# Swapping two returned parts of a KAN layer between TensorE's identity matmul and VectorE's sum

## The chip, the cores and the metric

The kernel runs on one core of one Trainium2 chip. The metric is the device time of one execution in microseconds (us). What is compared is the median over runs of the same kernel.

## The reference, cut to what matters

The program computes four layers in a row. The change lies in the third, a window layer made of "FastKAN" blocks over 8x8 windows of an image with 32 channels:

```python
def _fastkan(x, ln_g, ln_b, ws, wb, bb):
    ln = _layernorm(x, ln_g, ln_b)
    basis = jnp.exp(-((ln[..., None] - GRID) / DENOM) ** 2)      # 8 bases
    flat = basis.reshape(*basis.shape[:-2], -1)
    return flat @ ws.T + jax.nn.silu(x) @ wb.T + bb
y = _layernorm(wins, pn_g, pn_b)                                  # PN
a = y.reshape(b, WS, WS, c, S).transpose(0, 2, 3, 1, 4).reshape(b, WS * c, WS * S)
a = _fastkan(a, k1_ln_g, ...)                                     # K1
a = a.reshape(b, WS, c, WS, S).transpose(0, 3, 1, 2, 4).reshape(b, WS, WS, C)
d = y.reshape(b, WS, WS, c, S).transpose(0, 1, 3, 2, 4).reshape(b, WS * c, WS * S)
d = _fastkan(d, k2_ln_g, ...)                                     # K2
d = d.reshape(b, WS, c, WS, S).transpose(0, 1, 3, 2, 4).reshape(b, WS, WS, C)
e = _fastkan(y.reshape(b, WS * WS, C), k3_ln_g, ...).reshape(b, WS, WS, C)   # K3
z = a + d + e
z = _fastkan(z.reshape(b, WS * WS, C), k4_ln_g, ...).reshape(b, WS, WS, C)   # K4
out = z + wins
```

What matters here is `z = a + d + e`: the results of K1 and K2, which were computed in other layouts, are brought back and added to K3's.

## The kernel before, in words

The layer (`window_layer`) works on 64 tiles of 128 partitions x 2048 float32 values. Five engines run programs of their own, and each program is one static list. A table of positions at the top of the file (L1619 to L1642) gives each step of a tile a number; the steps of tile t stand at 128 t plus that number, and each engine issues its steps in the order of these sums. So several tiles are in flight: while K1, K2 and K3 of one tile are computed, K4 of the tile before is. One such period of 128 is called a round below.

In a round TensorE computes, for each of K1, K2, K3 and K4 in turn, eight basis products into the one accumulator `out` (`products`, L2144 to L2182). Some bases are ScalarE's exponentials (`ex`), the others are grown from them by VectorE with a multiplication by `ratio` (`grow`, L2018 to L2042). With the fifth product (`SILU_AT`) the silu part is added by four matmuls of 128x512 (L2173), and in K3, ahead of them, one of the two returned parts by four matmuls with the identity matrix (L2166). In the trace each 128x512 matmul of these is two records. Between the products stand the matmuls of the layer norms: centering (L2115, L2118), variance (L2128), spread (L2139).

K1 and K2 need their operands in other layouts. SyncE moves them by DMA from SBUF to SBUF, in eight transfers each: `feed_y` (L1812) brings the normed input into `kin`, `feed_u` (L1819) the silu operand into `ku`. K2's operands first pass a column-first copy on VectorE (`turn_y` L1958, `turn_u` L1963, tile `columns_first`). ScalarE evacuates K1's and K2's results over their silu operand in `ku` (`evacuate`, L1912), and `give_back` (L1828) moves them into B (`back_k1`, from K1) and D (`back_k2`, from K2). In B the columns are in the order of `out`. In D they are column-first: element (x, rw) of D belongs to element (rw, x) of `out`, with 8 x and 256 rw. The trace prints both as `back_k`; in the listing of the order, back_k_341 is B and back_k_335 is D.

After K3's last product, VectorE's `total` (L2007) adds three things into Z, K4's input: the accumulator, K3's bias, and the part that did not go through the identity matmul. Z, `out` and D are there read and written in D's order, so `out` and Z with a step of 8 elements.

All DMAs of the layer are SyncE's, in one list: besides the above, `load_x` (L1795, the next tile, from HBM), `load_r` (L1801, the tile again, for the residual) and `store` (L1806). Of the waits, these matter: `give_back` of K1 waits until K3's middle step of the tile before has read B, `give_back` of K2 until the total of the tile before has read D, both for their evacuation; `feed_u` waits until the last return of its kind has landed, since it overwrites what the return reads; K3's middle step waits for K1's return, the total for K2's.

Of the kernel before, what the change touches and what calls it, by code (L numbers as in the profile page):

```python
# [25 lines left out]
ALU = mybir.AluOpType  # L26
# [7 lines left out]
BAND = 8  # L34
BANDS = ROWS // BAND
TILE = BAND * COLS
BANK = 512
# [54 lines left out]
def wait_both(eng, sem_a, value_a, sem_b, value_b):  # L92

    value_a, value_b = (v if isinstance(v, int) else eng.to_reg(v) for v in (value_a, value_b))
    wait_past(eng, sem_a, value_a)
    wait_past(eng, sem_b, value_b)
# [1504 lines left out]
PN, K1, K2, K3, K4 = range(5)  # L1601
# [36 lines left out]
TANH, SILU = {PN: 231, K4: 449}, {PN: 241, K4: 452}  # L1638
TURN_Y, TURN_U, MEASURE = 230, 313, 633
LOAD_X, LOAD_R, STORE = 114, 552, 633  # L1640
FEED_Y, FEED_U, BACK = {K1: 218, K2: 235}, {K1: 261, K2: 328}, {K1: 365, K2: 421}
STAGES = 4  # L1642


# [34 lines left out]
def window_layer(net, k, source, bias, target, stats):  # L1679
    nc, c = net.nc, net.c  # L1680
# [11 lines left out]
    with ExitStack() as local:  # L1692
# [43 lines left out]
        def out_b(kind, h):  # L1736
            return k["end_b"][:, h:h + 1] if kind == K4 else vec[:, 3 * kind + 1:3 * kind + 2]

        def cols(n):
            return slice(BANK * n, BANK * n + BANK)  # L1740
# [4 lines left out]
        def after(t, first=1):  # L1745
            return not isinstance(t, int) or t >= first
# [38 lines left out]
        @block.sync  # L1785
        def _(sp):
            def chunks_first(tile_):
                return [tile_[:, cols(n)].rearrange("(g c) w -> c g w", g=GROUP) for n in range(CHUNKS)]

            def load_x(t, h):  # L1790
                pieces = chunks_first(source[band(t, h), h])
                if after(t):
                    sp.wait_ge(scaled[PN], t)
                for n in range(CHUNKS):
                    sp.dma_start(X[rows(n), :].rearrange("c (g w) -> c g w", g=GROUP), pieces[n]).then_inc(x_loaded, 16)  # L1795

            def load_r(t, h):
                pieces = chunks_first(source[band(t, h), h])
                wait_both(sp, stored, 16 * t, measured, t)
                for n in range(CHUNKS):  # L1800
                    sp.dma_start(R[rows(n), :].rearrange("c (g w) -> c g w", g=GROUP), pieces[n]).then_inc(r_loaded, 16)  # L1801

            def store(t, h):
                tile_ = target[band(t, h), h]
                sp.wait_ge(evacuated[K4], t + 1)
                sp.dma_start(tile_, R[:]).then_inc(stored, 16)  # L1806

            def feed_y(kind, t, h):
                wait_both(sp, normed if kind == K1 else copied_y, t + 1, exps, exps_done(kind, t - 1) if after(t) else 0)
                src = Y[:, h] if kind == K1 else turned[:]  # L1810
                for i in range(G):
                    sp.dma_start(kin[:, kind - K1, COLS * i:COLS * i + COLS],  # L1812
                                 src[P // G * i:P // G * i + P // G].rearrange("p (z n) -> p z n", z=BAND)).then_inc(kin_loaded[kind], 16)

            def feed_u(kind, t, h):
                wait_both(sp, u_ready[PN] if kind == K1 else copied_u, t + 1, back_loaded[kind], 128 * t)
                src = U[:, h] if kind == K1 else turned[:]
                for i in range(G):
                    sp.dma_start(ku[:, kind - K1, COLS * i:COLS * i + COLS],  # L1819
                                 src[P // G * i:P // G * i + P // G].rearrange("p (z n) -> p z n", z=BAND)).then_inc(ku_loaded[kind], 16)  # L1820

            def give_back(kind, t):
                if kind == K1:
                    wait_both(sp, used, BASES * slot_no(K3, t - 1) + (SILU_AT + 1) if after(t) else 0, evacuated[kind], t + 1)
                else:
                    wait_both(sp, summed, t, evacuated[kind], t + 1)
                for i in range(G):
                    sp.dma_start(back[kind][P // G * i:P // G * i + P // G].rearrange("p (z n) -> p z n", z=BAND),  # L1828
                                 ku[:, kind - K1, COLS * i:COLS * i + COLS]).then_inc(back_loaded[kind], 16)

            def round_(now):
                for u in range(UNITS):
                    for position, step in ((STORE, store), (LOAD_R, load_r), (LOAD_X, load_x)):
                        t, h = now.due(u, position)
                        if t is not None:
                            step(t, h)
                    for kind in (K1, K2):
                        t, h = now.due(u, FEED_Y[kind])
                        if t is not None:
                            feed_y(kind, t, h)  # L1840
                        t, h = now.due(u, FEED_U[kind])
                        if t is not None:
                            feed_u(kind, t, h)
                        t, h = now.due(u, BACK[kind])
                        if t is not None:
                            give_back(kind, t)
            rounds(sp, round_)
            sp.wait_ge(stored, 16 * TILES)
# [97 lines left out]
        def _(dve):  # L1946
            v = nc.vector

            def columns_first(tile_):
                return tile_.rearrange("p (x rw) -> p x rw", x=BAND)  # L1950

            def rows_first(tile_):
                return tile_.rearrange("p (rw x) -> p x rw", x=BAND)
# [48 lines left out]
            def total(t, h):  # L2002
                if after(t):
                    dve.wait_ge(exps, exps_done(K4, t - 1))
                dve.wait_ge(back_loaded[K2], 128 * t + 128)
                dve.wait_ge(used, BASES * slot_no(K3, t) + BASES)
                v.scalar_tensor_tensor(rows_first(Z[:]), rows_first(out_flat), out_b(K3, h), columns_first(D[:]), ALU.add,  # L2007
                                       ALU.add).then_inc(summed, 1)

            def measure(t, h):  # L2010
                dve.wait_ge(evacuated[K4], t + 1)
# [67 lines left out]
        def _(pe):  # L2079
# [63 lines left out]
            def products(kind, n, t, h):  # L2143
                if n == 0:  # L2144
                    last = slot_no.before(kind, t)
                    if last is not None:
                        pe.wait_ge(summed if last[0] == K3 else evacuated[last[0]], last[1] + 1)
                if n == SILU_AT:
                    if kind in (K1, K2):
                        pe.wait_ge(ku_loaded[kind], 128 * t + 128)  # L2150
                    else:
                        pe.wait_ge(u_ready[PN if kind == K3 else K4], t + 1)
                    if kind == K3:
                        pe.wait_ge(back_loaded[K1], 128 * t + 128)
                    elif kind == K4:
                        pe.wait_ge(r_loaded, 64 * t + 64)
                if n in ANCHORS[kind]:
                    pe.wait_ge(exps, exps_due)
                    pe.reg_add(exps_due, exps_due, 1)
                else:  # L2160
                    pe.wait_ge(grown, grown_due)
                    pe.reg_add(grown_due, grown_due, 1)
                if n == SILU_AT:
                    if kind == K3:
                        for i in range(CHUNKS):
                            m.matmul(out[:, i, :], c["ident"][:], B[:, cols(i)], start=False, stop=False)  # L2166
                    elif kind == K4:
                        for i in range(CHUNKS):
                            for g in range(GROUP):
                                m.matmul(out[rows(g), i, :], k["grown"][rows(i), h, rows(g)], R[rows(i), cols(g)],  # L2170
                                         start=False, stop=False, tile_position=(QUAD * i, QUAD * g))
                    for i in range(CHUNKS):
                        m.matmul(out[:, i, :], k["kan_silu"][:, kind - 1, :], silu_of(kind, h)[:, cols(i)], start=False, stop=False)  # L2173
                if n in ANCHORS[kind]:
                    base = ex[:, ANCHORS[kind].index(n)]
                else:
                    base = grown_ex[:, GROWTHS[kind].index(n) % GROWN]
                for i in range(CHUNKS):
                    for g in range(GROUP):
                        last = m.matmul(out[rows(i), g, :], k["kan_basis"][rows(g), kind - 1, n, :], base[rows(g), cols(i)],  # L2180
                                        start=(n == 0), stop=(n == BASES - 1), tile_position=(QUAD * g, QUAD * i))
                last.then_inc(used, 1)  # L2182
# [359 lines left out]
```

## Time and profile before

| | us |
|---|---|
| median of 3 runs | 10815.07 |
| lowest, highest | 10814.88, 10825.75 |
| the profiled execution: span from its first to its last instruction | 10821.2 |
| busy in it: TensorE | 8878.0 |
| VectorE | 8891.7 |
| ScalarE | 8014.9 |

A device time is listed for the runs and a span for the profiled execution; the span is what stands for that execution's own time here, and it lies among the three runs. The window layer's totals run from 4535 us to 10002 us of this span. Before it lie the two convolution layers with the residual and the pole layer, after it the pattern layer.

### The profile page before, as it was taken

To read this page: it belongs to the slowest core of one execution; us is meant where nothing else is said; L and a number is where in the kernel's file an instruction comes from. 1 tells how busy PE (TensorE), PEld (TensorE's weight loads), DVE (VectorE), ACT (ScalarE), POOL (GpSimd) and SP (SyncE) were. 2 spreads that over 40 slices of the span, in tenths; PEclk is the share of its full clock that TensorE was granted. 3 is DMA by queue.
4 is the path that set the end of the run, shared out by engine and by line. 5 is a ranking of instruction groups with operands and counts; after the bars stand their busy time and mean duration, and the time that the engine had idled before them with its cause. 6 is when DMAs were issued, how large, how long until landed. Compare 5 with 4: busy or idle time off the path is not lost. (4 is left out here: it accounts for less than half of the span.)

```text
span 10821.2 us, 354779 instructions
## 1 busy us (share of the span) xinstructions
PE 8878.0 (82%) x158376; PEld 4547.3 (42%) x158376; DVE 8891.7 (82%) x9022; ACT 8014.9 (74%) x5451; POOL 0.2 (0%) x4
## 2 busy tenths in 40 slices
PE   0889879996665799588888888888888888888788
PEld 0344434433442688244444444444344444443444
DVE  6777756666777588699999999999999999998788
ACT  0555545554552555599999999999999999998788
POOL 0000000000000000000000000000000000000000
PEclk9999989998887999699999999999999999999899
DMA  7999979996663588355444454555445455554576
GB/s 286 247 257 260 240 217 263 266 264 211 267 274 120 155 279 277 77 115 111 110 107 111 107 111 107 115 119 112 111 107 111 107 111 115 119 110 93 173 211 195
DMA packets 1196555, 1825.76 MB, mean 169 GB/s; under 512 B 135328, under 2 KB 956448, under 8 KB 1124768
## 3 DMA queue, kind: packets, MB, share of 16 engines
q1 hardware_dynamic: 1195040, 1803.05, 61.9%
q8 instruction: 1257, 20.59, 0.8%
q14 instruction: 258, 2.11, 0.1%
HBM read 717.78 MB, written 411.04 MB: 104 GB/s over the span
## 5 line engine op out<-in xcount | busy, mean ns | idle before, releaser
L2042 DVE SCALAR_TENSOR_TENSOR grown_ex<-ratio,ex 128x2048 f32<-128x2048 f32 x768 | 1756.1, 2287 | 229.7 <-PE out L2180 162.1
L2180 PE MATMUL out<-grown_ex,kan_basis 32*32 32x512 f32 x40960 | 1691.9, 625 | 7.7 <-DVE grown_ex L2042 5.4
L556 PE MATMUL conv<-uc,w 128*32 128x512 f32 x12288 | 1445.6, 596 | 15.4 <-DMA uc<-u 15.4
L1902 ACT ACTIVATE ex<-ex 128x2048 f32<-128x2048 f32 x768 | 1447.6, 1901 | 4.2
L2180 PE MATMUL out<-ex,kan_basis 32*32 32x512 f32 x24576 | 1233.3, 660 | 256.5 <-ACT ku L1912 156.5
L2042 DVE SCALAR_TENSOR_TENSOR grown_ex<-ratio,grown_ex 128x2048 f32<-128x2048 f32 x512 | 1171.2, 2288 | 27.4 <-PE out L2180 21.3
L463 ACT ACTIVATE v<-conv,cb 128x512 f32<-128x512 f32 x512 | 350.8, 685 | 899.6 <-PE conv L556 388.3
L2180 PEld LDWEIGHTS out<-grown_ex,kan_basis 32*32 32x32 f32 x40960 | 590.6, 106 | 731.1 <-issue 631.5
L1898 ACT ACTIVATE ex<-kin,offset 128x2048 f32<-128x2048 f32 x384 | 758.6, 1991 | 128.4 <-PE out L2180 127.8
L556 PEld LDWEIGHTS conv<-uc,w 128*32 128x32 f32 x12288 | 498.0, 109 | 715.7 <-issue 667.9
L2319 DVE TENSOR_TENSOR d<-xt 128x2313 f32<-128x2313 f32 (+2 forms) x256 | 621.7, 2495 | 88.2 <-PE acc L2373 87.9
L2373 PE MATMUL acc<-d,weights 32*32 32x512 f32 x16384 | 626.6, 599 | 73.3 <-issue 67.4
L2180 PEld LDWEIGHTS out<-ex,kan_basis 32*32 32x32 f32 x24576 | 419.6, 107 | 613.3 <-issue 532.5
L2139 PE MATMUL norm<-q,c_sel 32*128 32x128 f32 x10240 | 461.5, 328 | 171.5 <-ACT x L1863 136.6
L2139 PEld LDWEIGHTS norm<-q,c_sel 32*128 32x128 f32 x10240 | 391.8, 226 | 481.7 <-ACT x L1863 195.5
L2341 ACT ACTIVATE d<-d,steep 128x2313 f32<-128x2313 f32 (+2 forms) x256 | 534.0, 2159 | 35.3 <-DVE d L2319 35.3
L660 DVE TENSOR_TENSOR u<-xn,spread 128x512 f32<-128x512 f32 (+2 forms) x320 | 379.3, 1218 | 165.7 <-PE spread L521 163.5
L2128 PE MATMUL norm<-sq,c_kan_ones 128*32 128x128 f32 x10240 | 362.0, 281 | 176.3 <-ACT y L1865 76.0
L2173 PE MATMUL out<-ku,kan_silu 128*128 128x512 f32 x1024 | 472.6, 605 | 1.5 <-DVE grown_ex L2042 1.5
L2128 PEld LDWEIGHTS norm<-sq,c_kan_ones 128*32 128x32 f32 x10240 | 271.5, 112 | 464.8 <-issue 197.0
L2373 PEld LDWEIGHTS acc<-d,weights 32*32 32x32 f32 x16384 | 319.5, 103 | 327.7 <-issue 216.5
L1898 ACT ACTIVATE ex<-z,offset 128x2048 f32<-128x2048 f32 x192 | 383.2, 1996 | 54.5 <-PE out L2180 44.0
(287 smaller groups left out, 16012.2 us busy)
## 6 DMA issues: line engine op xcount, KB each, us to landing
uc<-u SPq DMA_DIRECT2D x2048, 129.0 KB, 3.5
xt<-in_x SPq DMA_DIRECT2D x128, 1024.0 KB, 7.3
t<-v SPq DMA_DIRECT2D x128, 1024.0 KB, 9.7
back_k<-ku SPq DMA_DIRECT2D x1024, 128.0 KB, 4.0
xt<-in_x SPq DMA_DIRECT2D x32, 2048.0 KB, 7.8
xt<-t SPq DMA_DIRECT2D x64, 1024.0 KB, 6.6
tt<-t SPq DMA_DIRECT2D x64, 1024.0 KB, 12.1
x<-x SPq DMA_DIRECT2D x64, 1024.0 KB, 4.9
```

Source lines behind the costliest of these rows:

```text
L556: last = m.matmul(conv[QUAD * b:QUAD * b + QUAD, k % 2, :], w_sb[:, o, d, :], uc[:, h, b, 2 * p:2 * p + 2, d:d + COLS], start=(d == 0), st ...
L660: return v.tensor_tensor(inside(u[:, h, first_row:first_row + rows, 1:COLS + 1]), inside(xn[:, h, at].rearrange("p (r w) -> p r w", w=COLS ...
L1898: a.activation(ex[:, j], norm_out(kind, h), ACT.Square, bias=k["offset"][:, kind - 1, n:n + 1]).then_inc(args, 1)
L1902: a.activation(ex[:, j], ex[:, j], ACT.Exp, scale=-1.0).then_inc(exps, 1)
L2042: v.scalar_tensor_tensor(grown_ex[:, at % GROWN], ratio[:], LARGEST, below, ALU.min, ALU.mult).then_inc(grown, 1)
L2128: last = m.matmul(norm[rows(quarter), 0, 0:P], k["c_kan_ones"][:, 0 if kind in (K1, K2) else 1, i, :], sq[:, block_:block_ + P], start=(i ...
L2139: last = m.matmul(norm[:, quarter, P * i:P * i + P], k["c_sel4"][rows(quarter), i, :], q[group][rows(quarter), group.index(kind), :], star ...
L2173: m.matmul(out[:, i, :], k["kan_silu"][:, kind - 1, :], silu_of(kind, h)[:, cols(i)], start=False, stop=False)
L2180: last = m.matmul(out[rows(i), g, :], k["kan_basis"][rows(g), kind - 1, n, :], base[rows(g), cols(i)], start=(n == 0), stop=(n == BASES - ...
L2319: v.tensor_tensor(d[:, h, n, rows, columns], there, xt[:, parity, h, rows, columns], ALU.subtract).then_inc(diff_ready, 1)
L2341: a.activation(t, t, ACT.Tanh, scale=steep[:, h:h + 1]).then_inc(tanh_ready, 1)
L2373: last = m.matmul(acc[quad(k), h, g, :], weights[quad(g), n, :], source_tile[quad(g), row + 2 * k:row + 2 * k + 2, column:column + COLS], ...
```

## The change

The two returned parts change places. K2's part (D) is now added inside K3 by the identity matmul, whose moving operand reads D with a step of 256 elements between neighbouring columns, so that its order becomes that of `out`. K1's part (B) is added by VectorE's total, in which all operands are now contiguous. The waits are exchanged accordingly, and K2's return gets position 383 in place of 421.

```diff
-FEED_Y, FEED_U, BACK = {K1: 218, K2: 235}, {K1: 261, K2: 328}, {K1: 365, K2: 421}
+FEED_Y, FEED_U, BACK = {K1: 218, K2: 235}, {K1: 261, K2: 328}, {K1: 365, K2: 383}
...
             def give_back(kind, t):
                 if kind == K1:
+                    wait_both(sp, summed, t, evacuated[kind], t + 1)
+                else:
                     wait_both(sp, used, BASES * slot_no(K3, t - 1) + (SILU_AT + 1) if after(t) else 0, evacuated[kind], t + 1)
-                else:
-                    wait_both(sp, summed, t, evacuated[kind], t + 1)
...
             def total(t, h):
...
-                dve.wait_ge(back_loaded[K2], 128 * t + 128)
+                dve.wait_ge(back_loaded[K1], 128 * t + 128)
                 dve.wait_ge(used, BASES * slot_no(K3, t) + BASES)
-                v.scalar_tensor_tensor(rows_first(Z[:]), rows_first(out_flat), out_b(K3, h), columns_first(D[:]), ALU.add,
-                                       ALU.add).then_inc(summed, 1)
+                v.scalar_tensor_tensor(Z[:], out_flat, out_b(K3, h), B[:], ALU.add, ALU.add).then_inc(summed, 1)
...
                     if kind == K3:
-                        pe.wait_ge(back_loaded[K1], 128 * t + 128)
+                        pe.wait_ge(back_loaded[K2], 128 * t + 128)
...
                     if kind == K3:
+                        by_rows = D[:].rearrange("p (x rw) -> p rw x", x=BAND)
                         for i in range(CHUNKS):
-                            m.matmul(out[:, i, :], c["ident"][:], B[:, cols(i)], start=False, stop=False)
+                            m.matmul(out[:, i, :], c["ident"][:], by_rows[:, BANK // BAND * i:BANK // BAND * i + BANK // BAND, :],
+                                     start=False, stop=False)
```

SyncE's list in a steady round, before (x at L1806 is the layer's output in HBM, written by the store; back_k_341 is K1's return, back_k_335 K2's):

```order
L1812 DMA kin<-columns_first 128x1x256 x8
L1828 DMA back_k_341<-ku 16x8x256 x8
L1795 DMA x<-x 32x4x512 x4
L1806 DMA x<-x_to_x_332 128x2048
L1819 DMA ku<-silu_y 128x1x256 x8
L1828 DMA back_k_335<-ku 16x8x256 x8
```

and now:

```order
L1812 DMA kin<-columns_first 128x1x256 x8
L1828 DMA back_k_341<-ku 16x8x256 x8
L1795 DMA x<-x 32x4x512 x4
L1806 DMA x<-x_to_x_332 128x2048
L1828 DMA back_k_335<-ku 16x8x256 x8
L1819 DMA ku<-silu_y 128x1x256 x8
```

K2's return has moved ahead of the feed of K1's silu operand for the next tile, and is directly behind the store. After both, in each list, comes the load for the residual.

TensorE's list around K3's middle step, with the semaphores that a row waits for, before (grown: a basis of VectorE's is ready; back_loaded1: K1's return has landed; u_ready0: the silu operand is ready; exps: an exponential is ready):

```order
L2128 MATMUL norm<-sq,c_kan_ones 32x128 x15
L2162 REGISTER_ALU [waits grown_394,back_loaded1_414,u_ready0_405]
L2166 MATMUL out<-back_k_341,c_ident 128x512 x4
L2173 MATMUL out<-silu_y,kan_silu 128x512 x4
L2180 MATMUL out<-grown_ex,kan_basis 32x512 x16
```

and now (back_loaded2: K2's return has landed):

```order
L2127 MATMUL norm<-sq,c_kan_ones 32x128 x15
L2161 REGISTER_ALU [waits grown_394,back_loaded2_415,u_ready0_405]
L2166 MATMUL out<-back_k_335,c_ident 128x512 x4
L2174 MATMUL out<-silu_y,kan_silu 128x512 x4
L2181 MATMUL out<-grown_ex,kan_basis 32x512 x16
```

The place of the identity matmuls is the same; the return that they wait for, and the tile that they read, are the other ones.

## Rows read from the trace of the kernel before

**Rows 1.** The page's head and busy time by engine.

```profile
span 10821.2 us, 354779 instructions
...
PE 8878.0 (82%) x158376; PEld 4547.3 (42%) x158376; DVE 8891.7 (82%) x9022; ACT 8014.9 (74%) x5451; POOL 0.2 (0%) x4
```

**Rows 2.** One line's view: L2007, the total; ns min/median/max, first and last start.

```profile
L2007 DVE SCALAR_TENSOR_TENSOR z<-out,kan_vec,back_k x64: 3893/3946/3999, 4535.0 to 9998.1; 128x2048 f32<-128x2048 f32 x64
```

**Rows 3.** Timeline of VectorE, one round: start us, us, what, idle before.

```profile
7019.58 2.03 DVE L1958 COPY columns_first<-y 128x2048 f32<-128x2048 f32 x1
...
7050.07 2.29 DVE L2042 SCALAR_TENSOR_TENSOR grown_ex<-ratio,ex 128x2048 f32<-128x2048 f32 x1 [1.68 <-PE out L2180]
...
7055.01 3.94 DVE L2007 SCALAR_TENSOR_TENSOR z<-out,kan_vec,back_k 128x2048 f32<-128x2048 f32 x1 [0.39 <-ACT ex L1902]
...
7072.31 2.29 DVE L2042 SCALAR_TENSOR_TENSOR grown_ex<-ratio,ex 128x2048 f32<-128x2048 f32 x1 [0.31 <-PE out L2180]
...
7104.77 2.03 DVE L1958 COPY columns_first<-y 128x2048 f32<-128x2048 f32 x1
```

**Rows 4.** Windows, second round: busy time by engine, granted clock, DMA share, GB/s.

```profile
7996.00:8001.00 5.00, 4.71 (x51) 2.52 (x52) 3.92 (x6) 4.47 (x4) 0.00 (x0) 0.66 0.99 326
```

**Rows 5.** Timeline of TensorE in the second round.

```profile
7996.29 1.09 PE L2180 MATMUL out<-ex,kan_basis 32*32 32x512 f32 x16 [2.02 <-issue]
7997.31 1.94 PE L2128 MATMUL norm<-sq,c_kan_ones 128*32 128x128 f32 x32
7999.18 4.45 PE L2166 MATMUL out<-back_k,c_ident 128*128 128x512 f32 x8
```

**Rows 6.** Timeline of VectorE in the second round.

```profile
7974.89 2.03 DVE L1958 COPY columns_first<-y 128x2048 f32<-128x2048 f32 x1
...
8009.48 2.29 DVE L2042 SCALAR_TENSOR_TENSOR grown_ex<-ratio,ex 128x2048 f32<-128x2048 f32 x1 [5.11 <-PE out L2180]
```

**Rows 7.** Timeline of TensorE in the first round.

```profile
7039.51 1.08 PE L2128 MATMUL norm<-sq,c_kan_ones 128*32 128x128 f32 x32 [0.42 <-ACT sq L1872]
7040.52 3.70 PE L2166 MATMUL out<-back_k,c_ident 128*128 128x512 f32 x8
...
7058.11 1.65 PE L2139 MATMUL norm<-q,c_sel 32*128 32x128 f32 x32 [2.19 <-ACT x L1863]
7059.68 2.01 PE L2180 MATMUL out<-ex,kan_basis 32*32 32x512 f32 x32
...
7083.48 3.70 PE L2173 MATMUL out<-ku,kan_silu 128*128 128x512 f32 x8
```

**Rows 8.** Timeline of SyncE's issues in the first round.

```profile
7021.64 5.15 SPq L1812 DMA_DIRECT2D kin<-columns_first  x8
7026.89 5.44 SPq L1828 DMA_DIRECT2D back_k<-ku  x8
7032.37 3.40 SPq L1795 DMA_DIRECT2D x<-x  x4
7035.81 0.43 SPq L1806 DMA_DIRECT2D x<-x_to_x  x1
7036.34 8.39 SPq L1819 DMA_DIRECT2D ku<-silu_y  x8
```

**Rows 9.** Lines' views: K1's return from 7026.8, then the silu feed's last issue.

```profile
DMA to landing us min/median/max: 3.3/3.4/4.4
...
L1819 SPq DMA_DIRECT2D ku<-silu_y x1: 599/599/599, 7044.1 to 7044.1; - x1
...
DMA to landing us min/median/max: 3.8/3.8/3.8
```

**Rows 10.** Timeline of ScalarE: K2's evacuation in the first round.

```profile
7030.15 1.96 ACT L1912 ACTIVATE ku<-out,kan_vec 128x2048 f32<-128x2048 f32 x1
```

**Rows 11.** Groups by line and shape, 5000 to 9800 us: busy, mean ns, idle before.

```profile
L1991 DVE SCALAR_TENSOR_TENSOR kin<-kin,kan_vec,norm 128x2048 f32<-128x2048 f32 x110 | 257.4, 2340 | 0.0
...
L1958 DVE COPY columns_first<-y 128x2048 f32<-128x2048 f32 x56 | 113.8, 2032 | 0.0
```

## The prediction, made before the changed kernel ran

> **What bounds the kernel now.** I read the profile in this order: the page, to see which engines fill the span; the single line of the instruction that the change rewrites; one round of the layer on SyncE, on TensorE, on VectorE and on ScalarE; then a second round, in which chance delayed TensorE.
>
> The span is 10821.2 us, and TensorE and VectorE are each busy for 82% of it [rows 1]. The change touches the KAN stage alone. Its 64 totals start between 4535.0 and 9998.1 us [rows 2], so a round lasts (9998.1 - 4535.0) / 63 = 86.7 us on average. The round that I read is a quiet one: VectorE's column-first copy starts at 7019.58 and again at 7104.77 [rows 3], 85.2 us later. In it VectorE is nearly always at work, with a wait of 1.68 us ahead of 7050.07 as the longest in the rows shown, and that wait ends on TensorE's K3 products [rows 3]. So inside this stretch TensorE is already the later of the two, by 1.68 us, and anything that delays TensorE ahead of that point reaches VectorE in full.
>
> The second round shows this happening. TensorE stood still for 2.02 us at 7996.29 before it reached K3's middle step. It then ran at a lower granted clock (0.66 over 7996 to 8001, so partly at 1.2 GHz), the variance matmuls took 1.94 us and the four identity matmuls (eight records) 4.45 us, and VectorE waited 5.11 us where it otherwise waits 1.68 [rows 4 to 6]. The quiet round has 3.70 us for the same identity matmuls [rows 7]. From the end of the column-first copy to the identity matmuls are 7999.18 - 7976.92 = 22.26 us there and 7040.52 - 7021.61 = 18.91 us in the quiet round [rows 3, 5, 6, 7]: TensorE came 3.35 us later, and VectorE's wait grew by 3.43 us.
>
> **The change, part by part.**
>
> 1. K3's middle step now needs K2's return, not K1's. K1's return starts at 7026.89, is issued in 5.44 us, and its eight transfers land 3.3 to 4.4 us after issue [rows 8, 9], all of them by 7032.3 + 4.4 = 7036.7, which is 3.8 us ahead of the identity matmuls at 7040.52. K2's part is far later: ScalarE's evacuation of it runs from 7030.15 to 7032.11 [rows 10]. It is then ready, but SyncE is not. SyncE's chain starts when VectorE's column-first copy ends (7021.61) and runs without a pause: K2's feed 5.15 us, K1's return 5.44, the load of x 3.40, the store 0.43 [rows 8]. Even at its new, earlier place K2's return is issued no sooner than 7036.3. Today the feed of K1's silu operand stands exactly there, with the same eight transfers of 128 KB: SyncE takes 8.39 us to issue them, behind the megabyte load and the megabyte store, and the last one, issued at 7044.1, lands 3.8 us later, at 7047.9 [rows 8, 9]. I price K2's return by this row, since it will stand in the same queue behind the same work. TensorE would be kept 7047.9 - 7040.5 = 7.4 us. The average round is 1.5 us longer than this one, largely because TensorE arrives late in some, and there the stall hides as much; I take 1.0 us off: **+6.4 us** a round. Bounds: with the eight issues at the 5.44 us of K1's return and 3.4 us of landing the last arrives at 7045.1, a stall of 4.6, and 3.6 with the same 1.0 off; with a landing 2 us later than the row, 8.4.
> Nothing can be put in the stall's place: TensorE takes its instructions in order, and behind the wait stand K3's silu matmuls, its last four products, the spread for K2 and x's centering. The step from the identity matmuls to VectorE's release is 7050.07 - 7040.52 = 9.55 us of unbroken TensorE work [rows 3, 7].
>
> 2. The clock. After the chance gap of 2.02 us the variance matmuls took 0.86 us longer than the 1.08 of the quiet round and the identity matmuls 0.75 us longer [rows 5, 7]: 1.6 us of loss behind a gap that is a third of the new stall. **+1.6 us** a round; bounds 0 and 3.2 (twice that, if the lower clock lasts twice as long).
>
> 3. The identity matmuls themselves. Their moving operand now steps by 256 elements (1 KB) from one column to the next. No matmul of the trace reads so. The nearest row is VectorE's column-first copy, which reads SBUF with a step of 8 elements: 2032 ns for 2048 elements, about 1 ns each, less than the 2340 ns of the contiguous form below [rows 11]. TensorE takes 3.70 us for 8 x 512 columns, 0.9 ns each, nearly the same pace, so I take **0**. Bounds: 0 (it cannot be quicker than the contiguous read) and 3.7, a doubling.
> The Trainium skill ("SBUF — State Buffer", in the section on the DMA port swizzle) says that SBUF is read in lines of 16 bytes and that each access that crosses to a new line pays a penalty. The copy row does not bear this out for VectorE; no run here shows it for TensorE, and by that rule the upper bound would be the value to take.
>
> 4. VectorE's total. It reads PSUM and writes Z with a step of 8 elements today; plain and contiguous it should cost what the scale step costs, one PSUM operand and one SBUF operand in 2340 ns [rows 11]; it takes 3.94 us today [rows 3]. That is 1.6 us of VectorE's time a round. Most of it is not on the path. The total ends at 7055.01 + 3.94 = 7058.95, while TensorE's next work waits for ScalarE's x until 7058.11, then spreads for 1.65 us, and opens K4 at 7059.68 [rows 3, 7]. VectorE waits again for TensorE's K4 products at 7072.31, 0.31 us [rows 3]. An earlier end of the total would mostly lengthen that wait. **-0.4 us** a round; bounds 0 and -1.6.
>
> 5. SyncE. K2's return moves ahead of K1's silu feed and of R's load; both keep their number of transfers, and the silu feed now lands some 6 us later. It is needed only at K1's middle step of the next tile, whose silu matmuls start at 7083.48 [rows 7], near 30 us after it lands, so I put 0 on it. The exchanged waits of the two returns (the last total, the last middle step of K3) are both from the tile before and long past: 0.
>
> Sum: 6.4 + 1.6 + 0 - 0.4 = 7.6 us a round, times 64 tiles = 486 us. On the profiled execution's 10821.2 us that is 11307; this execution's span lies 6 us above the median of the three runs, 10815.07, so against the median it is 11301, and I say **11300 us**.
>
> **Rivals.**
>
> A. *K2's return lands in time, and the change is faster.* The mechanism: the return goes out the moment that ScalarE has evacuated K2, at 7032.1. Eight issues at 0.65 us and 3.4 us of landing end at 7040.7, within 0.2 us of the identity matmuls. It decides at a landing 18.9 us after the copy's end. Then only the total's gain is left, 0.4 to 1.6 us a round: 26 to 103 us, 10712 to 10790. Against it stand the load of x and the store, which hold SyncE until 7036.3 [rows 8]. Chance 0.05.
>
> B. *The strided operand costs as well.* Doubling the identity matmuls adds 3.7 us x 64 = 237 us to the forecast: 11537. Against it is the copy row; for it, that the step is 1 KB and no row has that on TensorE. It is the time that the Trainium skill's rule on SBUF lines would give. Chance 0.2.
>
> C. *The stall is absorbed.* If the rounds had slack elsewhere (SyncE's chain starting earlier against TensorE, ScalarE running ahead), the stall would show only as a longer wait and the time would stay within 0.2%, about what a measurement of this kernel can tell from no change. The second round speaks against it: 3.35 us of delay came out as 3.43 us of waiting. Chance 0.04, with 10795 to 10835.
>
> D. *The forecast*, a stall of 4 to 8 us a round and little else: chance 0.71.
>
> **How the numbers follow.** The low end takes a stall of 3.6 us, a clock loss of 1.6 and a gain of 0.4: 4.8 x 64 = 307, so 11120. The high end takes 8.4 + 3.2 less 0.4, or 6.4 + 1.6 + 3.7 for rival B with its price: 11.2 to 11.7 x 64 = 717 to 749, so 11560. What lies outside is A, C and a slim tail above. Faster by more than 0.2% has A's 0.05, within 0.2% C's 0.04, slower the rest, 0.91.
>
> **What the changed profile would show.** Right: rounds of 93 to 96 us; TensorE idle 5 to 8 us before the identity matmuls, ended by the DMA of K2's return; VectorE's wait before K4's first growth 8 to 10 us in place of 1.68; a total of about 2.34 us; the granted clock at its lower level behind the stall; the window's DMA work unchanged. The identity matmuls stay at 3.7 us (5.3 with the lower clock) if the stride is free. Wrong: K2's return landing less than 19 us after the copy; identity matmuls of 7 us at the full clock; or a stall on TensorE without longer rounds.

## The result, and the profile after

| | before | changed |
|---|---|---|
| median, us | 10814.97 (4 runs) | 11641.49 (4 runs) |
| lowest to highest | 10807.23 to 10825.75 | 11621.33 to 11646.12 |
| ratio | | 1.0757, 95% interval 1.0737 to 1.0776 |

The change costs 826 us, 12.9 us for each of the 64 tiles. The direction was as forecast; the size was 1.7 times the forecast 485 us, and the time lies above the stated range. In the sessions of the experiments below the kernel before had medians of 10815 to 10847 us, so each experiment is read by its ratio to the kernel before in its own session.

The page of the changed kernel: head, busy time, the two groups that grew, and the issues of the returns (size, median us to landing).

```profile
span 11644.3 us, 354779 instructions
...
PE 9107.5 (78%) x158376; PEld 4588.8 (39%) x158376; DVE 8795.3 (76%) x9022; ACT 8016.7 (69%) x5451; POOL 0.2 (0%) x4
...
L2041 DVE SCALAR_TENSOR_TENSOR grown_ex<-ratio,ex 128x2048 f32<-128x2048 f32 x768 | 1756.4, 2287 | 1043.3 <-PE out L2181 988.2
...
L2166 PE MATMUL out<-back_k,c_ident 128*128 128x512 f32 x512 | 463.5, 1061 | 603.2 <-issue 603.2
...
back_k<-ku SPq DMA_DIRECT2D x1024, 128.0 KB, 8.9
```

VectorE is 96 us less busy than in [rows 1], which is the cheaper total, and the kernel is 826 us slower. Its growths from an exponential (L2041) now wait 1043 us, 988 of them for TensorE, where they waited 230. The identity matmuls are preceded by 603 us of idle TensorE; and TensorE itself is busy for 230 us more, 64 x 3.6 us.

One round on SyncE, in answer to [rows 8]:

```profile
7093.32 5.15 SPq L1812 DMA_DIRECT2D kin<-columns_first  x8
7098.57 6.71 SPq L1828 DMA_DIRECT2D back_k<-ku  x8
7105.32 2.04 SPq L1795 DMA_DIRECT2D x<-x  x4
7107.40 0.43 SPq L1806 DMA_DIRECT2D x<-x_to_x  x1
```

K2's return follows at 7107.95, 14.6 us after the end of the column-first copy (7093.30), as forecast. The line's view of single issues of that return, first and last, and of the silu feed behind it, first and seventh:

```profile
L1828 SPq DMA_DIRECT2D back_k<-ku x1: 552/552/552, 7108.0 to 7108.0; - x1
DMA to landing us min/median/max: 8.6/8.6/8.6
...
L1828 SPq DMA_DIRECT2D back_k<-ku x1: 598/598/598, 7114.7 to 7114.7; - x1
DMA to landing us min/median/max: 7.8/7.8/7.8
...
L1819 SPq DMA_DIRECT2D ku<-silu_y x1: 601/601/601, 7115.4 to 7115.4; - x1
DMA to landing us min/median/max: 7.1/7.1/7.1
...
L1819 SPq DMA_DIRECT2D ku<-silu_y x1: 607/607/607, 7119.3 to 7119.3; - x1
DMA to landing us min/median/max: 5.6/5.6/5.6
```

The last transfer of the return lands 7.8 us after its issue, at 7122.5, where the silu feed that stood in this place before landed 3.8 us after its own [rows 9]. The eight returns land between 7116.6 and 7122.5, one every 0.84 us. The feed's first seven land between 7122.5 and 7124.9, one every 0.40 us; its eighth, issued at 7120.0, takes 6.6 us and lands at 7126.6.

TensorE in that round, in answer to [rows 7]:

```profile
7111.97 1.08 PE L2127 MATMUL norm<-sq,c_kan_ones 128*32 128x128 f32 x32 [0.42 <-ACT sq L1872]
7122.87 7.24 PE L2166 MATMUL out<-back_k,c_ident 128*128 128x512 f32 x8 [9.82 <-issue]
7129.93 3.61 PE L2174 MATMUL out<-silu_y,kan_silu 128*128 128x512 f32 x8
```

VectorE, in answer to [rows 3]:

```profile
7091.26 2.04 DVE L1958 COPY columns_first<-y 128x2048 f32<-128x2048 f32 x1
...
7135.96 2.29 DVE L2041 SCALAR_TENSOR_TENSOR grown_ex<-ratio,ex 128x2048 f32<-128x2048 f32 x1 [15.11 <-PE out L2181]
...
7140.89 2.35 DVE L2007 SCALAR_TENSOR_TENSOR z<-out,kan_vec,back_k 128x2048 f32<-128x2048 f32 x1 [0.38 <-ACT ex L1902]
...
7149.12 2.29 DVE L2041 SCALAR_TENSOR_TENSOR grown_ex<-ratio,grown_ex 128x2048 f32<-128x2048 f32 x1 [1.48 <-PE out L2181]
```

TensorE idles 9.8 us, and VectorE waits 15.1 us where it waited 1.7. The total takes 2.35 us instead of 3.94, and the third growth behind it, which had no wait in the round read before, now waits 1.48 us for TensorE: nearly all of the 1.6 us saved is given back at once.

The windows over the stall (us, busy by engine with counts, granted clock, DMA share, GB/s):

```profile
7112.00:7116.00 4.00, 1.05 (x32) 0.78 (x32) 3.74 (x3) 3.52 (x2) 0.00 (x0) 1.00 1.02 335
7116.00:7120.00 4.00, 0.00 (x0) 0.00 (x0) 3.45 (x8) 3.95 (x3) 0.00 (x0) 0.67 1.13 163
7120.00:7124.00 4.00, 1.13 (x2) 0.62 (x3) 0.77 (x2) 3.54 (x2) 0.00 (x0) 0.50 1.11 251
7124.00:7128.00 4.00, 4.00 (x6) 1.43 (x5) 0.00 (x0) 0.00 (x0) 0.00 (x0) 0.55 1.08 227
7128.00:7132.00 4.00, 4.00 (x8) 1.37 (x7) 0.00 (x0) 0.00 (x0) 0.00 (x0) 1.00 0.37 74
```

While the return lands (7116 to 7120) the DMA engines are occupied throughout and move only 163 GB/s; and the first 5 us of the identity matmuls fall under a granted clock near 0.5, which is 1.2 GHz.

### The profile page after: what moved, and what is told of

Its sections match the earlier page's. It is cut to its first block and busy times, and to the rows that moved or that the text cites. A ratio compares the mean times of both kernels' runs of the same rounds, so it can differ in the third digit from the quotient of the medians.

```text
span 11644.3 us, 354779 instructions
## 1 busy us (share of the span) xinstructions
PE 9107.5 (78%) x158376; PEld 4588.8 (39%) x158376; DVE 8795.3 (76%) x9022; ACT 8016.7 (69%) x5451; POOL 0.2 (0%) x4
## 5 line engine op out<-in xcount | busy, mean ns | idle before, releaser
L2041 DVE SCALAR_TENSOR_TENSOR grown_ex<-ratio,ex 128x2048 f32<-128x2048 f32 x768 | 1756.4, 2287 | 1043.3 <-PE out L2181 988.2
L2041 DVE SCALAR_TENSOR_TENSOR grown_ex<-ratio,grown_ex 128x2048 f32<-128x2048 f32 x512 | 1170.8, 2287 | 120.3 <-PE out L2181 115.6
L2166 PE MATMUL out<-back_k,c_ident 128*128 128x512 f32 x512 | 463.5, 1061 | 603.2 <-issue 603.2
L2166 PEld LDWEIGHTS out<-back_k,c_ident 128*128 128x128 f32 x512 | 140.3, 289 | 837.0 <-issue 837.0
```

The costliest lines, as they stand in the source:

```text
L2041: v.scalar_tensor_tensor(grown_ex[:, at % GROWN], ratio[:], LARGEST, below, ALU.min, ALU.mult).then_inc(grown, 1)
L2166: m.matmul(out[:, i, :], c["ident"][:], by_rows[:, BANK // BAND * i:BANK // BAND * i + BANK // BAND, :], start=False, stop=False)
```

## The experiments

Two readings carry the comparison. *Arrival* is the time from the end of VectorE's column-first copy to the first identity matmul. *Release* is the time from there to the start of VectorE's first K4 growth. Both, and the *round* (total to total), are means over tiles 3 to 61 of the timelines of each run's profile.

| kernel | arrival | identity matmuls | release | round | time, us | ratio to before (95%) |
|---|---|---|---|---|---|---|
| before | 20.0 | 3.8 | 9.7 | 86.9 | 10815 | |
| changed | 29.5 | 7.2 | 13.1 | 99.9 | 11641 | 1.076 (1.074 to 1.078) |
| e1 return at 366 | 22.9 | 7.2 | 13.0 | 93.3 | 11246 | 1.039 (1.037 to 1.041) |
| e6 return at 371 | 27.2 | 7.2 | 13.1 | 97.6 | 11505 | 1.061 (1.056 to 1.067) |
| e7 return at 421 | 32.5 | 7.2 | 13.1 | 103.0 | 11843 | 1.093 (1.087 to 1.099) |
| e5 return shaped as a feed | 26.0 | 7.2 | 13.1 | 96.3 | 11418 | 1.053 (1.048 to 1.059) |
| e2 operand plain | 29.5 | 5.8 | 11.6 | 98.6 | 11558 | 1.068 (1.066 to 1.070) |
| e8 at 366, operand plain | 22.7 | 4.9 | 10.7 | 91.0 | 11112 | 1.025 (1.019 to 1.031) |
| e3 before, operand strided | 19.9 | 7.2 | 13.0 | 90.2 | 11048 | 1.021 (1.019 to 1.023) |
| e4 before, total plain | 19.8 | 3.8 | 9.7 | 86.6 | 10816 | 0.999 (0.998 to 1.000) |
| e12 before, step of 16 bytes | 19.9 | 7.5 | 13.3 | 90.6 | 11075 (one run) | |
| e11 before, step of 8 bytes | 20.0 | 3.9 | 9.8 | 87.2 | 10864 (one run) | |

In every row the round is 86.9 plus what arrival and release have above 20.0 and 9.7, to within 0.4 us: the changed kernel, 86.9 + 9.5 + 3.4 = 99.8 against 99.9; e8, 86.9 + 2.7 + 1.0 = 90.6 against 91.0. Next to nothing is left over for the total. Where TensorE waits for the return (the changed kernel, e1, e2, e5 to e8), its last landing lies 0.1 to 0.2 us ahead of the arrival, both as means of each run's trace, so the arrival is that landing. e9 and e10 move the identity matmuls behind two more products; the two readings mean something else there, and they stand below and not in the table.

The theory after the result, as the expectations below call it, is **S**: a late return and a slow operand are two separate costs, each in full on the path. Its rivals (the letters are not those of the prediction): **C**, that the 7.2 us of the identity matmuls are the lower clock; **V**, that VectorE's total counts; **Q**, that only the queue ahead makes the return late.

**e1, the return ahead of the load and the store.**

```diff
-... BACK = ..., {K1: 365, K2: 383}
+... BACK = ..., {K1: 365, K2: 366}
```

> The changed kernel with one number altered: K2's return at position 366 instead of 383, so directly behind K1's return and ahead of the load of x and of the store. Theory S (the lateness of the return and the strided operand are two separate costs): the last transfer lands 20.5 to 21.5 us after the end of the column-first copy instead of 29.3, TensorE's gap before the identity matmuls falls from 9.7 us to 0.5 to 2, the identity matmuls stay at 7.24 us; a round of 90.5 to 92 us, a time of 11050 to 11150 us. Theory C (the 7.24 us are the lower clock after the gap and the stride is free): with the gap gone the identity matmuls are back at 3.7 us and the time is 10830 to 10900 us.

Timeline of TensorE, then of SyncE, one round:

```profile
7053.85 7.21 PE L2166 MATMUL out<-back_k,c_ident 128*128 128x512 f32 x8 [3.89 <-issue]
```

```profile
7029.71 5.15 SPq L1812 DMA_DIRECT2D kin<-columns_first  x8
7034.96 12.75 SPq L1828 DMA_DIRECT2D back_k<-ku  x16
7047.75 2.04 SPq L1795 DMA_DIRECT2D x<-x  x4
```

The arrival falls from 29.5 to 22.9 us and the identity matmuls stay at 7.2, which speaks against C. It does not settle it: a gap of 3.2 us on average is left, and the granted clock over these matmuls is still 0.77 on average. e3 settles it. The arrival is later than the 21.5 us that I allowed and the time 96 us above S's range: 16 returns in a row take longer than I allowed (on average K2's eight are issued over 5.3 us and land over 6.6). A place ahead of K1's return was not tried. K2's evacuation ends 10.5 us after the copy [rows 3, 10] and its return starts 11.4 us after it here, so that place could start it at most some 0.9 us sooner.

**e2, the stride taken out of the changed kernel** (K2's part is then added in the wrong column order).

```diff
-    m.matmul(out[:, i, :], c["ident"][:], by_rows[:, ...], ...)
+    m.matmul(out[:, i, :], c["ident"][:], D[:, cols(i)], ...)
```

> The changed kernel with D read contiguously by the identity matmuls (K2's part is then added in the wrong column order). All waits and all DMAs stay. Theory S: TensorE's gap stays at 9 to 10 us; the lower clock, which in the changed kernel covers about the first 5 us after the gap, becomes visible, so the identity matmuls take 5 to 6.5 us; time 11520 to 11600 us. Theory C: the stride cost nothing, so the identity matmuls stay at 7.2 us and the time at 11640 us.

TensorE, one round:

```profile
7093.06 6.07 PE L2166 MATMUL out<-back_k,c_ident 128*128 128x512 f32 x8 [10.35 <-issue]
```

The stall stays, the matmuls take 5.8 us on average and the time falls by 83 us, inside S's range. So behind a stall the lower clock costs 5.8 - 3.8 = 2.0 us. In the changed kernel it costs nothing more, because the strided matmuls take 7.24 to 7.25 us in every round from tile 3 to 61, though their granted clock is 0.69 on average. The two costs overlap.

**e3, the stride alone, in the kernel before** (K1's part in the wrong column order): the identity matmuls read B as the change reads D.

> The kernel before, with one edit: the identity matmuls read B with the step of 256 elements (K1's part is then added in the wrong column order). Nothing waits for anything else than before. Theory S: the identity matmuls take 7.2 us instead of 3.7 in every round, at the full clock too, and all of it is on the path: (7.24 - 3.70) x 64 = 227 us, time 11020 to 11060 us. Theory C: the stride is free, 10815 us.

The line's view of the identity matmuls (ns min/median/max), and under it the same view before:

```profile
L2167 PE MATMUL out<-back_k,c_ident x512: 1041/1044/1223, 4530.1 to 10209.7; 128*128 128x512 f32 x171
```

```profile
L2166 PE MATMUL out<-back_k,c_ident x512: 590/593/1223, 4521.1 to 9985.9; 128*128 128x512 f32 x171
```

With no stall and no changed wait the stride costs 3.3 us a round and 2.1% of the time. In 53 of the 59 rounds from tile 3 to 61 the full clock was granted over all of these matmuls, and there they take 7.2 us. So C falls.

**e4, the total alone, in the kernel before** (K2's part in the wrong column order).

```diff
-    v.scalar_tensor_tensor(rows_first(Z[:]), rows_first(out_flat), out_b(K3, h), columns_first(D[:]), ...)
+    v.scalar_tensor_tensor(Z[:], out_flat, out_b(K3, h), D[:], ...)
```

> The kernel before, with one edit: the total reads the accumulator and D and writes Z contiguously (K2's part is then added in the wrong column order). Theory P (the total is not on the path): the total takes 2.35 us instead of 3.95, VectorE waits for TensorE's first K4 products instead, and the time falls by 0 to 25 us. Theory V (VectorE is the bound): it falls by 1.6 x 64 = 102 us, to 10713 us.

The line's view, then the waits between 5400 and 9600 us (us in total, times, longest), here and before:

```profile
L2007 DVE SCALAR_TENSOR_TENSOR z<-out,kan_vec,back_k x64: 2345/2350/2352, 4541.3 to 9982.6; 128x2048 f32<-128x2048 f32 x64
```

```profile
DVE grown_ex L2041 <- PE out L2179: 211.0, 143, 6.4
```

```profile
DVE grown_ex L2042 <- PE out L2180: 145.5, 107, 5.7
```

VectorE saves 1.6 us a round in work and waits 66 us more over some 48 rounds, 1.4 us each. The time is the same within the interval, so V falls.

**e5, the return with a feed's shape.** Each of its eight transfers reads 16 partitions and writes 128, the other way about (D's arrangement is then another).

```diff
-    sp.dma_start(back[kind][P // G * i:P // G * i + P // G].rearrange("p (z n) -> p z n", z=BAND),
-                 ku[:, kind - K1, COLS * i:COLS * i + COLS])
+    sp.dma_start(D[:, COLS * i:COLS * i + COLS],      # K2 alone
+                 ku[P // G * i:P // G * i + P // G, 1].rearrange("p (z n) -> p z n", z=BAND))
```

> The changed kernel, K2's return still at 383, but each of its eight transfers now reads 16 partitions and writes all 128, as a feed does, instead of reading 128 and writing 16 (D then holds K2's part in another arrangement). Number, size (128 KB) and row length (1 KB) of the transfers stay. Theory W (the return is slow by its own shape; in the changed kernel one of its transfers lands every 0.80 us, one of the silu feed's every 0.40): the spacing falls to 0.4 to 0.5 us and the last one lands 25.5 to 27 us after the column-first copy instead of 29.3; TensorE's gap is 6.5 to 7.5 us, the time 11400 to 11500 us. Theory Q (only the queue ahead of it, with the load of x and the store, makes it late): no change, 11640 us.

TensorE, one round:

```profile
7023.57 7.24 PE L2170 MATMUL out<-back_k,c_ident 128*128 128x512 f32 x8 [6.81 <-issue]
```

The arrival falls by 3.5 us at the same place in the queue, with the same bytes in rows of the same length, so Q falls as the sole cause. As means over tiles 3 to 59, the first of the eight transfers lands 22.2 us after the copy and the last 25.8; in the changed kernel it is 23.3 and 29.3. So 1.1 us of the 3.5 lie ahead of the first landing and 2.4 in the pace of the eight: the first seven land 0.40 us apart here and 0.80 there. Whether it is the reading of 128 partitions or the writing of 16 that is slow was not separated.

**e6 and e7, other places for the return.** 371 is between the load of x and the store, 421 the old place.

> The changed kernel with K2's return at position 371: behind the load of x, ahead of the store. With 366 (ahead of both) the last transfer landed 22.7 us after the column-first copy, with 383 (behind both) 29.3. Theory Q2 (each of the two megabytes ahead costs about its own transfer time): 25.5 to 26.5 us, a time of 11400 to 11470 us. Rival (the store alone does it): 23 to 24 us and 11250 to 11320 us.

> The changed kernel with K2's return left at its old position, 421, behind the feed of K1's silu operand. This is the exchange without the move. Theory S (each us of landing later is a us of the round): the last transfer lands 33 to 37 us after the column-first copy, the round grows to 104 to 108 us and the time to 11900 to 12150 us. Rival (the rounds have slack that takes up a longer stall): under 11750 us.

The line's view of the returns' issues between 7000 and 7110 us, at 371 and then at 421 (in both stretches only K2's return has landings on record).

```profile
DMA to landing us min/median/max: 6.5/7.1/7.5
```

```profile
DMA to landing us min/median/max: 3.3/3.4/3.6
```

In these two rounds a transfer takes 7.1 us to land behind the megabyte load and 3.4 behind the silu feed. Over 5400 to 9600 us the medians are 7.6 and 4.0, so the second round is a quick one: on average e7's eight returns are issued over 4.7 us and land over 6.0.

The arrival is 22.9 us ahead of both large transfers, 27.2 behind the load, 29.5 behind both, 32.5 behind the silu feed too. By these differences the load of x costs 4.3 us, more than I gave it, and the store 2.3; e6 missed my range upward by 35 us, e7 missed it downward by 57, since the silu feed costs only 3.0. The new place that came with the change saves 1.6% against leaving the return where it was (1.093 to 1.076), and every place tried is slower than before.

**e8, early and plain together** (K2's part in the wrong column order).

> The changed kernel with K2's return at 366 and D read contiguously (K2's part is then added in the wrong column order): the exchange with its stride removed and its lateness cut to what two returns in a row need. Theory S: TensorE's gap stays near 3.2 us, the identity matmuls take 4 to 6 us (part of them at the lower clock), the round 90.5 to 92 us, the time 11050 to 11150 us: still slower than before, since the total's 1.6 us are not on the path. Theory V (the total's 1.6 us count once TensorE no longer loses time to the stride): 10950 us or less.

Inside S's range. The exchange loses 2.5% even without its stride, from 2.7 us of later arrival and 1.0 us of lower clock.

**e9, the need made later.** e1's kernel with K3's middle step at the seventh product instead of the fifth.

```diff
-    SILU_AT = BASES // 2
+    SILU_AT = {K1: BASES // 2, K2: BASES // 2, K3: BASES // 2 + 2, K4: BASES // 2}
```

> The changed kernel with K2's return at 366 and K3's middle step (its wait for the return, the identity matmuls and the silu matmuls) moved from its fifth to its seventh product. Two products of about 0.9 us each then run before the wait. Theory S: TensorE's gap falls from 3.2 to about 1.4 us and that is gained in each round: 91.3 to 92 us, time 11120 to 11180 us, still slower than before by the stride's 3.4 us a round. Rival (VectorE's wait only moves to the spread behind the seventh product, and the sum of the path stays): 11246 us as with 366 alone.

11117.53 us, ratio 1.025 (1.022 to 1.029) against 1.039 in e1, and just below S's range. TensorE's gap falls to 0.6 us. It is the fastest form of the exchange found that adds every part in its right order, and still slower than before.

**e10, the same edit in the kernel before**, meant as a version faster than both.

> The kernel before with the same edit: K3's middle step at the seventh product instead of the fifth. TensorE does the same work in the same total time; only the sixth product, which releases VectorE's first K4 growth, comes 7.3 us earlier. Theory M (what VectorE needs next is the spread behind the seventh product, at the same time as before): 0 to 20 us faster. Rival N (the wait of 1.7 us before the growth is what bounds the round): up to 1.7 x 64 = 109 us faster, 10706 us.

Wrong for both theories: 10955.35 us, ratio 1.010 (1.007 to 1.013). VectorE, one round:

```profile
6564.06 2.29 DVE L2042 SCALAR_TENSOR_TENSOR grown_ex<-ratio,ex 128x2048 f32<-128x2048 f32 x1 [0.98 <-ACT ex L1902]
...
6567.93 2.35 DVE L1991 SCALAR_TENSOR_TENSOR kin<-kin,kan_vec,norm 128x2048 f32<-128x2048 f32 x1 [1.57 <-PE norm L2139]
...
6570.92 3.98 DVE L2007 SCALAR_TENSOR_TENSOR z<-out,kan_vec,back_k 128x2048 f32<-128x2048 f32 x1 [0.65 <-ACT ex L1902]
```

In place of the waits of 1.68 and 0.39 us [rows 3] stand three, of 3.2 us together, and the identity matmuls start 24.2 us after the copy, on average, where two products more should have made it 21.8. In that stretch TensorE is idle for 3.7 us on average, against 2.9 before, and its granted clock is 0.96 against 0.99. One reading is that the 7.3 us of identity and silu matmuls were cover under which ScalarE and VectorE made K3's next bases, and that they cover nothing once they are moved behind. It is argued from these rows and not shown.

**e11 and e12, how large a step costs.** The kernel before, with the identity matmuls reading B with a step of 2 and of 4 elements (K1's part in the wrong column order).

```diff
-    m.matmul(..., B[:, cols(i)], ...)
+    m.matmul(..., B[:].rearrange("p (n s) -> p s n", s=2)[:, i // 2, cols(i % 2)], ...)      # e11
+    m.matmul(..., B[:].rearrange("p (n s) -> p s n", s=4)[:, i, :], ...)                     # e12
```

> The kernel before with the identity matmuls reading B with a step of 2 elements, 8 bytes (K1's part is then added in the wrong column order). Theory L (a read pays when consecutive elements lie in different lines of 16 bytes): two elements share a line, so 3.7 to 4.0 us for the identity matmuls and 10815 us. Theory T (any step but 1 pays): 7.2 us and about 11040 us.

> The kernel before with the identity matmuls reading B with a step of 4 elements, 16 bytes (K1's part is then added in the wrong column order). Theory L: each element lies in a line of its own, so 7.2 us and about 11040 us, as with a step of 1 KB. Rival (only large steps pay): 3.7 us, 10815 us.

The line's view of each, step 8 bytes and then 16:

```profile
L2166 PE MATMUL out<-back_k,c_ident x512: 609/611/1222, 4528.7 to 10016.9; 128*128 128x512 f32 x171
```

```profile
L2166 PE MATMUL out<-back_k,c_ident x512: 1078/1079/1250, 4530.4 to 10237.8; 128*128 128x512 f32 x171
```

593 ns contiguous, 611 at 8 bytes, 1079 at 16 bytes, 1044 at 1 KB: the cost comes between 8 and 16 bytes and is no larger at 1 KB. Steps between these were not run.

## Why the prediction was right or wrong

**The bound and the mechanism of the stall: right.** TensorE stands still at K3's middle step until K2's return has landed; VectorE waits for it; each us of it is a us of the round. Four places of the return (e1, e6, the change, e7) show it over arrivals of 22.9 to 32.5 us. The prediction's rivals A (the return lands in time) and C (the stall is absorbed) fall with that. Its rival B (the strided operand costs as well) came true on top of the stall.

**Step 1, the stall: the term was mis-sized.** I put 6.4 us with 8.4 as the upper bound; it is 9.5. The start of the return, 14.6 us after the copy, was right, and so was the 1.0 us taken off for the rounds in which TensorE arrives late: the arrival before is 20.0 us on average and 18.9 in the round that I read. Wrong was "I price K2's return by this row, since it will stand in the same queue behind the same work": the row was a feed. A return has the same bytes and the same number of transfers but goes from 128 partitions to 16. With a feed's shape at the same place the arrival is 3.5 us earlier (e5), which covers the 3.1 us by which I missed. K1's return stood in my own rows with 3.4 us from issue to landing, and the low bound and rival A took it as the price of a return; but it had no large load and store ahead of it, and that round was a quick one: as means over tiles 3 to 59 before, its eight transfers are issued over 5.1 us, land over 6.5, and the last takes 5.0 us.

**Step 2, the clock: right in size, wrong in the sum.** A stall costs 2.0 us of lower clock with a plain operand (e2), against 1.6 forecast. In the changed kernel it is covered by the stride.

**Step 3, the strided operand: wrong.** I took 0 from VectorE's copy and kept 3.7 for the upper bound. It is 3.4 to 3.5 us, nearly the doubling. Identity matmuls of 7 us at the full clock were named as a sign of being wrong, and e3 shows them. The rule that I set aside, of the Trainium skill ("SBUF — State Buffer", in the section on the DMA port swizzle), that each access to a new line of 16 bytes pays, is what the runs show on TensorE: 3% at 8 bytes, where two elements share a line, 82% at 16 bytes and 76% at 1 KB. The Trainium skill gives in the same section four float32 elements as the reach of a free step. On TensorE a step of four elements pays in full (e12), and the measurement decides. A row of one engine was no evidence on another's read path, and I read even that row wrongly. I held the copy's 2032 ns against an operation with two sources. The contiguous operation with one source in the same window, L1995 over the same 2048 elements, takes 1287 ns:

```profile
L1995 DVE TENSOR_SCALAR y<-y,kan_vec 128x2048 f32<-128x2048 f32 x56 | 72.0, 1287 | 2.0
```

So the copy row did not show that a step of 8 elements is free on VectorE. The total, 3.94 us with steps against 2.34 without, stood in my rows as well, and I used it for step 4 only.

**Step 4, the total: right in kind.** Forecast -0.4 of a possible -1.6; it is 0 within what e4 can tell (-0.2% to 0, at most 0.3 us a round), for the reason given: VectorE's next wait on TensorE takes it back.

**Step 5, SyncE: right.** The silu feed's last transfer lands 5.5 us later after the copy (32.8 against 27.3 on average), and TensorE does not wait for it: ahead of the silu matmuls that read `ku` it is idle for 1.4 us in the whole changed run.

**The sum.** 9.5 + 3.4 = 12.9 us a round, times 64 = 826 us, the measured difference. The forecast 7.6 missed 3.1 us in step 1 and 3.4 in step 3, and counted 1.6 for the clock and -0.4 for the total, which do not show in the time. **The range** failed because its high end took the long stall or the strided operand, each against the central value of the other. Both happened, and the stall of 9.5 us is past its own upper bound as well.

## What to carry to other kernels

Price a moved DMA by the same transfer, with its partitions on both sides and what stands ahead of it in the queue, not by one of the same size: here eight transfers of 128 partitions into 16 took 14.9 us from the first issue to the last landing, and of 16 into 128 at the same place 11.5 (e5). When an operand moves to another engine, its access pattern has to be priced on that engine: TensorE read float32 with a step of 8 bytes 3% slower than contiguously, and with steps of 16 bytes and of 1 KB at little more than half the speed. A row that is to show that a step is free has to be held against the same kind of operation without the step. And before an engine's work is made cheaper, find its next wait: 1.6 us a round, saved between two waits on TensorE, came to nothing.

## What the runs showed of the hardware that I had not expected

- TensorE's float32 matmul of 128x512 takes 593 ns a record with a contiguous moving operand, 611 with a step of 8 bytes, 1079 with 16 and 1044 with 1 KB. VectorE's copy with a step of 32 bytes takes 2032 ns for 2048 elements [rows 11], and a contiguous operation with one source 1287 (L1995); no contiguous copy of that size was run.
- The strided matmuls take 7.2 us in all, whether at the full clock (e3) or with about 5 us of them at a granted clock near 0.5 (the changed kernel): the slow read hides the slow clock. With a plain operand the clock shows, 5.8 us against 3.8 (e2).
- SBUF to SBUF, behind the load of x and the store, of eight transfers of 128 KB in rows of 1 KB the first seven land 0.80 us apart from 128 partitions into 16 (the changed kernel) and 0.40 us apart from 16 into 128 (e5); the eighth comes 1.2 us after the seventh in both. Ahead of the load and the store, K1's returns before are issued 0.73 us apart and the first seven land 0.86 apart. All are means over tiles 3 to 59.
